# Cross-attention keys as a split product in rows, copied and turned, in place of an fp32 product

## The chip, the cores and the metric

The kernel runs on one core of one Trainium2 chip. The metric is the device time of one launch in microseconds (us), as the median of several runs. The engines are named as the profile names them: PE (TensorE; PEld is its weight loads), DVE (VectorE), ACT (ScalarE), POOL (GpSimd) and SP (SyncE, which issues most DMAs).

## The reference

```python
x = x + cross_attn(layernorm(x), ctx_1024, key_bias, key_mask, Wq, Wkv, out_w)   # 16 heads of 32, softmax over keys
x = x + self_attn(layernorm(x), Wq, Wk, Wv, Wo)       # 128 tokens; q, k, v, weights and outputs clipped to [1e-7, 1 - 1e-7]
x = x + experts(layernorm(x), gate_w, w1, w2)         # each of 8 experts picks 32 of 128 tokens; 512 -> 2048, gelu, -> 512
```

x is 4 x 128 x 512 in fp32, the context 4 x 2048 x 512. In the cross-attention, keys are `ctx @ Wk.T + bk` and values `ctx @ Wv.T + bv`. The padded tail of each batch's context is masked out.

## The kernel before, in words

The program has one hand-written instruction list for each engine, with semaphores between them. Every engine executes its own list in order, so an instruction that waits holds everything behind it on its engine.

The work goes in three parts: an **opening** (layer norm, query projection, splitting of weights), a **chunk loop** over blocks of 128 context rows (with this mask and `ctx_s` loaded 11 times, 11 chunks are needed), and then the self-attention and the experts. Chunk 0 is written out, chunks 1 to 8 run in a hardware loop (`Fori(1, prev)`), chunk 9 (`prev`, with `at_end=True`) is written out with extra normalisations between its steps, and chunk 10 (`last`) is interleaved with the output projection.

Most products are **split products**. A factor a is stored as a_hi (rounded to fp32r, by ACT, in `w_hi`, `tr_hi`, `ctx_hi`) and a_lo = a - a_hi (by DVE, in `w_lo`, `tr_lo`, `ctx_lo`), and the product is three fp32r passes: hi x hi, hi x lo, lo x hi. `w_hi` and `w_lo` have four slots of a 512 x 512 weight each; `att_w` has eight places for raw weights (`wq_s, wk_s, wv_s, wo_s, sq_s, sk_s, sv_s, so_s`). Later the expert weights are loaded into the same eight places.

In the body for chunk t, PE's list (`chunk` in the tensor block) runs:

- `k_project(t + 1)`: the keys of the next chunk. 16 fp32 matmuls of 128 columns, weight stationary, so the keys come out with the head dimension on the partitions, in the PSUM bank `pk`.
- `turn_values(t)`: four transposes of the previous chunk's output, copied by ACT to `ot_s`.
- `v_project(t + 1, k)` for k = 0 to 3: three fp32r matmuls of 512 columns each into the PSUM bank `pv`, a split product with `ctx_hi`/`ctx_lo` stationary. Between them `turn_probs(t, c)`, transposes of the exponentials.
- `scores(t + 1)`: bias matmuls (L1395) and 16 small products (L1400), then `values(t)` (L1420).

DVE's list for chunk t: `maximum(t, nm, 0)`, `maximum(t, nm, 1)` (row maxima of the scores, L908), `v_evacuate(t)` (L843, it frees `pv` for `v_project(t + 1)`), `split_chunk(t + 1)` (L849, `ctx_lo`), `moved_maxima` (L916, L918), `k_evacuate(t + 1)` (L854, adds the bias and writes `kt_s`), `add_values` (L937), `turned_probs` (L930) for c = 0, 1, then `rescale` (L925), `turned_probs` for c = 2, and `add_sums`. `scores(t + 1)` overwrites the banks that `turned_probs` reads, so it waits for the third of these (`pt_dve`) and for ACT's copy (`pt_act`). `v_project(t + 1, 0)` waits for `v_out`, which `v_evacuate(t)` raises.

ACT's list for chunk t: `split_chunk(t + 1)` (L543, `ctx_hi`, waits for `v_mm`, the end of the previous `v_project`), `turned_out`, 16 exponentials (L488) and `turned_last`.

Of the kernel before, what the change touches and what calls it, by code (L numbers as in the profile page):

```python
# [38 lines left out]
def decoder_layer(nc, x, ctx_t, key_bias, key_mask, wq, wk, wv, bv, wo, bo, bias_cols,  # L39
                  sq, sk, sv, sbv, so, sbo, gate, w1, w2, out):  # L40
    with ExitStack() as ctx:
# [11 lines left out]
        ot_s = att_w[:, 6, 0].rearrange("p (k t) -> p k t", k=KC)  # L53
# [126 lines left out]
        att_hi_ok = sem("att_hi_ok"); att_lo_ok = sem("att_lo_ok")  # L180
# [21 lines left out]
        norm_hi_ok = sem("norm_hi_ok"); norm_lo_ok = sem("norm_lo_ok"); last_lo_ok = sem("last_lo_ok"); last_mm = sem("last_mm"); last_out = sem("last_out"); last_resid = sem("last_resid"); ones_ok = sem("ones_ok"); resid_ok = sem("resid_ok"); first_hi_ok = sem("first_hi_ok"); first_lo_ok = sem("first_lo_ok");  spread_ok = sem("spread_ok")  # L202
# [10 lines left out]
        x_now_ok = sem("x_now_ok"); xin_hi_ok = sem("xin_hi_ok"); xin_staged = sem("xin_staged"); back_staged = sem("back_staged")  # L213
# [5 lines left out]
        SPLITS = ((wv_s, 1, in_wv), (sv_s, 3, in_sv), (wo_s, 2, in_wo), (sq_s, 1, in_sq), (sk_s, 0, in_sk), (so_s, 1, in_so))  # L219
# [70 lines left out]
        def _(sp):  # L290
# [45 lines left out]
            for i in range(2 * NQ):  # L336
# [4 lines left out]
                if i == 6:  # L341
                    sp.wait_ge(bt_mm, last + 1)
# [20 lines left out]
        def _(pool):  # L363
# [42 lines left out]
            g.memset(ones[:], 1.0).then_inc(ones_ok, 1)  # L406
# [64 lines left out]
        def _(act):  # L471
# [114 lines left out]
            split_att(3)  # L586
# [5 lines left out]
            split_att(4)  # L592
# [5 lines left out]
            split_att(5)  # L598
# [164 lines left out]
        def _(dve):  # L763
# [124 lines left out]
            part_split(1, 0, 2)  # L888
# [957 lines left out]
```

## Time and profile before

| | |
|---|---|
| median of 3 runs | 454.85 us (454.65 to 454.88) |
| the profiled execution, its own time | 455.0 us |
| its span, first to last instruction | 453.3 us |
| granted TensorE clock, mean | 0.996 of full |
| PE busy | 437.7 us, 97% |
| DVE busy | 367.4 us, 81% |
| ACT busy | 302.1 us, 67% |
| POOL busy | 86.9 us, 19% |
| one iteration of the chunk loop | 11.11 us |

Busy shares are averages over the whole span. The time outside of the span is 1.7 us. What a change in one part is worth is read from that part: which wait ends last there.

### The profile page before, as it was taken

How to read it: one execution, taken by the hardware profiler on the slowest of the kernel's cores; microseconds unless marked ns; L12 is line 12 of the kernel's file. 1: busy time of each engine (PE TensorE's matmuls, PEld its weight loads, DVE VectorE, ACT ScalarE, POOL GpSimd, SP SyncE). 2: the span in 40 equal slices, each digit the busy share in tenths (PEclk: the TensorE clock that was granted, in tenths of full speed). 3: DMA queues.
4: the chain of work that ended last, by engine and by line, in shares of the span. 5: the costliest groups of instructions: out<-in, count | busy, mean ns of one | idle time of the engine just before them, and what ended most of it. 6: DMA issues, size and time to landing. Idle time of an engine off the chain costs nothing.

```text
span 453.3 us, 9856 instructions
## 1 busy us (share of the span) xinstructions
PE 437.7 (97%) x3424; PEld 363.9 (80%) x3424; DVE 367.4 (81%) x516; ACT 302.1 (67%) x622; POOL 86.9 (19%) x111
## 2 busy tenths in 40 slices
PE   7999999999998999999998999999999999999995
PEld 3888888888886789878877787878778787878795
DVE  6889777777778876668987989888989898998972
ACT  4557666666665643667274877787777878778852
POOL 6100000000000122000142150505041230505002
PEclk9999999999999999999998999999999999999999
DMA  8980000001010921800000499999999989999102
GB/s 257 386 296 26 25 23 23 23 23 23 23 26 22 331 99 61 269 12 3 1 0 1 161 387 387 387 387 387 384 324 353 357 310 354 298 357 300 55 1 93
DMA packets 43105, 82.02 MB, mean 181 GB/s; under 512 B 2632, under 2 KB 3784, under 8 KB 43080
## 3 DMA queue, kind: packets, MB, share of 16 engines
q1 hardware_dynamic: 41816, 81.09, 51.3%
q10 hardware_dynamic: 1264, 0.59, 0.5%
q8 instruction: 16, 0.26, 0.2%
q14 instruction: 9, 0.07, 0.0%
HBM read 80.57 MB, written 1.10 MB: 180 GB/s over the span
## 4 chain that ended last, share of the span: by engine, by line
PE 84%; DVE 9%; ACT 2%; issue 2%; DMA 1%; POOL 1%; DVEq 1%; SPq 0%; POOLq 0%
PE po L1689 18%; PE pk L1689 11%; PE pv L1689 10%; PE pk L1298 8%; PE pv L1308 5%; PE ps L1327 5%; PE po L1715 3%; PE ps L1407 3%; PE pv L1327 3%; PE ps L1452 3%; PE ps L1400 2%; PE po L1420 2%; PE pk L1327 1%; PE po L1327 1%; DMA x_s<-in_x 1%
## 5 line engine op out<-in xcount | busy, mean ns | idle before, releaser
L1234 DVE TENSOR_TENSOR w_lo<-att_w,w_hi 128x2048 fp32r<-128x2048 f32 x60 | 138.0, 2309 | 21.3 <-ACT w_hi L705 21.3
L705 ACT CAST w_hi<-att_w 128x2048 fp32r<-128x2048 f32 x60 | 115.1, 1918 | 15.5 <-PE po L1689 15.5
L488 ACT ACTIVATE big_a<-ps,negm 128x128 f32<-128x128 f32 x176 | 62.3, 396 | 0.0
L1689 PE MATMUL po<-w_hi,ht_hi 128*128 128x512 f32 (+1 forms) x128 | 50.0, 391 | 0.0
L1689 PE MATMUL po<-w_hi,ht_lo 128*128 128x512 f32 (+1 forms) x128 | 48.7, 380 | 0.0
L1689 PE MATMUL po<-w_lo,ht_hi 128*128 128x512 f32 (+1 forms) x128 | 48.6, 380 | 0.0
L1298 PE MATMUL pk<-ctx_s,att_w 128*128 128x128 f32 x352 | 42.1, 278 | 0.0
L1298 PEld LDWEIGHTS pk<-ctx_s,att_w 128*128 128x128 f32 x352 | 40.2, 192 | 1.9 <-issue 1.8
L488 ACT ACTIVATION_READ_ACCUMULATOR big_a<-ps,negm 128x1 f32 x176 | 41.4, 235 | 0.0
L908 DVE TENSOR_REDUCE mc<-ps 128x8 f32<-128x1024 f32 x22 | 26.9, 1221 | 10.4 <-PE ps L1400 10.3
L1689 PEld LDWEIGHTS po<-w_hi,ht_lo 128*128 128x128 f32 x128 | 24.0, 187 | 5.1
L1689 PEld LDWEIGHTS po<-w_lo,ht_hi 128*128 128x128 f32 x128 | 24.1, 188 | 4.4
L1689 PEld LDWEIGHTS po<-w_hi,ht_hi 128*128 128x128 f32 x128 | 24.0, 188 | 4.4
L425 POOL COPY q_now<-qk 128x512 f32 x10 | 6.1, 613 | 110.9 <-PE ps L1400 110.9
L456 POOL CAST back_now<-state 128x128 fp32r (+1 forms) x8 | 8.6, 1070 | 95.9 <-PE ps L1734 87.5
L1689 PE MATMUL pk<-w_hi,xin_hi 128*128 128x512 f32 x64 | 26.2, 409 | 0.0
L1689 PE MATMUL pv<-w_hi,xin_hi 128*128 128x512 f32 x64 | 25.9, 405 | 0.0
L1689 PE MATMUL pk<-w_hi,xin_lo 128*128 128x512 f32 x64 | 25.3, 395 | 0.0
L1689 PE MATMUL pk<-w_lo,xin_hi 128*128 128x512 f32 x64 | 25.2, 394 | 0.0
L1689 PE MATMUL pv<-w_lo,xin_hi 128*128 128x512 f32 x64 | 25.2, 394 | 0.0
L1689 PE MATMUL pv<-w_hi,xin_lo 128*128 128x512 f32 x64 | 25.2, 394 | 0.0
L1407 PEld LDWEIGHTS ps<-ident,big_a 128*128 128x128 f32 x176 | 21.2, 140 | 4.3
(348 smaller groups left out, 1023.9 us busy)
## 6 DMA issues: line engine op xcount, KB each, us to landing
att_w<-in_w SPq DMA_DIRECT2D x64, 1024.0 KB, 7.2
ctx_s<-in_ctx_t SPq DMA_DIRECT2D x11, 256.0 KB, 2.7
x_s<-in_x SPq DMA_DIRECT2D x4, 256.0 KB, 4.2
att_w<-in_wk SPq DMA_DIRECT2D x1, 1024.0 KB, 7.8
att_w<-in_wq SPq DMA_DIRECT2D x1, 1024.0 KB, 10.3
att_w<-in_wv SPq DMA_DIRECT2D x1, 1024.0 KB, 13.5
att_w<-in_sv SPq DMA_DIRECT2D x1, 1024.0 KB, 16.1
att_w<-in_wo SPq DMA_DIRECT2D x1, 1024.0 KB, 15.8
```

The costliest lines, as they stand in the source:

```text
L488: ins = a.activation(big_a[:, h], ps[:, c, g * P:(g + 1) * P], ACT.Exp, bias=negm[:, h:h + 1], accum_out=sums[:, h:h + 1])
L705: a.copy(w_hi[:, i % SLOTS], att_w[:, i]).then_inc(hi_ok, 1)
L908: v.tensor_reduce(mc[:, hs], ps[:, 2 * half:2 * half + 2].rearrange("p c (g k) -> p (c g) k", k=P), AX.X, ALU.max).then_inc(loop_dve, 1)
L1234: v.tensor_tensor(w_lo[:, i % SLOTS], att_w[:, i], w_hi[:, i % SLOTS], ALU.subtract).then_inc(lo_ok, 1)
L1298: ins = mm(pk[:, g * P:(g + 1) * P], wk_s[:, k, g * P:(g + 1) * P], ctx_s[:, k], start=k == 0, stop=k == KC - 1)
L1308: ins = mm(pv[:], c[:, k], w[:, 1, k], start=k == 0 and c is ctx_hi and w is w_hi, stop=k == KC - 1 and c is ctx_lo, skip_group_check=True)
L1327: ins = mm(dst, l, r, start=n == 0, stop=n == len(pairs) - 1, skip_group_check=True)
L1400: ins = mm(ps[:, c, g * P:(g + 1) * P], q_now[r, g], kt_s[r, g], start=False, stop=True, skip_group_check=True)
L1407: ins = nc.tensor.transpose(ps[:, c, g * P:(g + 1) * P], big_a[:, c * KC + g], ident[:])
L1452: ins = mm(banks[g], w[:, 2, k, g * P:(g + 1) * P], t[:, k], start=first and k == 0, stop=end and k == KC - 1, skip_group_check=True)
L1689: ins = mm(dst, l, r, start=start and i == 0, stop=i == len(terms) - 1, skip_group_check=True)
L1715: ins = nc.tensor.transpose(po[:, 1, c * P:(c + 1) * P], h_s[:, q % 2, c * P:(c + 1) * P], ident[:])
```

## The change

The keys of chunks 1 to 10 become a split product too. The context is now stationary and the weight moves (12 fp32r matmuls of 512 columns), so the keys come out with the context rows on the partitions. DVE copies that from `pk` to `k_rows` (a part of the place of `wq_s`), PE turns it back with four transposes into `pk` (`k_turn`), and `k_evacuate` follows as before. Chunk 0 keeps its fp32 product.

For that the key weight is split in the opening into slot 3, in the place where the self-attention's value weight was split. The high half of that weight is now made by ACT after the softmax of chunk 9, its low half by POOL (`sv_lo_ok`) in four parts. In the opening DVE's additions of the output bias to `x_s` are spread out. On DVE `split_chunk(t + 1)` moves ahead of the second `maximum`, and in SP's list the wait for `k_mm` ahead of the load of the next chunk falls away. The order of the first expert's weight loads changes.

```diff
+        k_rows = att_w[:, 0, 1]
...
-        SPLITS = ((wv_s, 1, in_wv), (sv_s, 3, in_sv), (wo_s, 2, in_wo), (sq_s, 1, in_sq), (sk_s, 0, in_sk), (so_s, 1, in_so))
+        SPLITS = ((wk_s, 3, in_wk), (wv_s, 1, in_wv), (wo_s, 2, in_wo), (sv_s, 3, in_sv), (sq_s, 1, in_sq), (sk_s, 0, in_sk), (so_s, 1, in_so))
...
                 load_bias(t)
-                sp.wait_ge(k_mm, t + 1)
                 sp.wait_ge(ctx_lo_ok, t + 1)
                 load_chunk(t + 1)
...
-            for i in range(2 * NQ):
+            for i in (1, 2, 3, 6, 0, 4, 5, 7):
+                if i == 6:
+                    sp.wait_ge(sv_lo_ok, KC)
+                if i == 0:
+                    sp.wait_ge(bt_mm, last + 1)
...
+            pool.wait_ge(att_hi_ok, 4)
+            for k in range(KC):
+                g.tensor_tensor(w_lo[:, 3, k], sv_s[:, k], w_hi[:, 3, k], ALU.subtract).then_inc(sv_lo_ok, 1)
             shifts(1)
...
             split_chunk(last)
             softmax_chunk(prev, True)
+            act.wait_ge(kr_mm, last)
+            split_att(3)
             transposed(1, 0)
...
+            def k_copy(t):
+
+                dve.wait_ge(kr_mm, t)
+                v.tensor_copy(k_rows, pk[:]).then_inc(kr_out, 1)
...
-            dve.wait_ge(in_bo, 16)
-            for b in range(B):
-                ins = v.tensor_tensor(x_s[:, b], x_s[:, b], bo_b[:], ALU.add)
-            link(ins)
             split_att(0)
+            split_att(1)
...
+            output_bias(0, 1)
...
-            part_split(1, 0, 2)
+            output_bias(1, 2)
...
                 maximum(t, nm, 0)
+                split_chunk(t + 1)
                 maximum(t, nm, 1)
                 if before is not None:
                     dve.wait_ge(pv_mm, t)
                 v_evacuate(t)
-                split_chunk(t + 1)
                 moved_maxima(t, nm)
                 if before is None:
-                    part_split(1, 2, 4)
-                k_evacuate(t + 1)
+                    output_bias(2, 4)
+                k_copy(t + 1)
                 if before is not None:
                     add_values(before, t)
                 else:
                     part_split(2, 0, 1)
                 turned_probs(t, 0)
+                k_evacuate(t + 1)
...
             def k_project(t):
-                pe.wait_ge(ctx_in, t * 16 + 16)
-                if not isinstance(t, int) or t > 0:
-                    pe.wait_ge(k_out, t)
+
+                pe.wait_ge(ctx_hi_ok, t + 1)
+                pe.wait_ge(k_out, t)
+                for w in (w_hi, w_lo):
+                    for k in range(KC):
+                        mm(pk[:], ctx_hi[:, k], w[:, 3, k], start=w is w_hi and k == 0, stop=False, skip_group_check=True)
+                pe.wait_ge(ctx_lo_ok, t + 1)
+                for k in range(KC):
+                    ins = mm(pk[:], ctx_lo[:, k], w_hi[:, 3, k], start=False, stop=k == KC - 1, skip_group_check=True)
+                ins.then_inc(kr_mm, 1)
+
+            def k_turn(t):
+
+                pe.wait_ge(kr_out, t)
                 for g in range(KC):
-                    ins = k_block(t, g)
+                    ins = nc.tensor.transpose(pk[:, g * P:(g + 1) * P], k_rows[:, g * P:(g + 1) * P], ident[:])
                 ins.then_inc(k_mm, 1)
...
                 turn_probs(t, 0)
+                k_turn(t + 1)
                 v_project(t + 1, 1)
...
             def values_project(b):
 
+                pe.wait_ge(sv_lo_ok, KC)
                 pe.wait_ge(tr_lo_ok[2], b + 1)
```

How it moves instructions, on PE, at the head of the loop's body. Before (L1298 is the key product, L1428 `turn_values`, L1308 `v_project`, L1407 `turn_probs`):

```order
L1298 MATMUL pk<-ctx_s,att_w 128x128 [waits k_out,ctx_in]
L1298 MATMUL pk<-ctx_s,att_w 128x128 x15
L1428 MATMUL po<-ident,att_w 128x128 [waits ot_out]
L1428 MATMUL po<-ident,att_w 128x128 x3
L1304 REGISTER_ALU
L1308 MATMUL pv<-w_hi 128x512 [waits v_out,ctx_lo_ok]
L1308 MATMUL pv<-w_lo,w_hi 128x512
L1308 MATMUL pv<-w_hi,w_lo 128x512
L1405 ISA
L1407 MATMUL ps<-ident,big_a 128x128 [waits p_ok]
```

The same place in the changed kernel (its lines are numbered anew: L1311 and L1314 are the key product, L1459 `turn_values`, L1339 `v_project`, L1438 `turn_probs`, L1321 `k_turn`), from the second third of the key product on:

```order
L1311 MATMUL pk<-w_lo,w_hi 128x512 x4
L1314 MATMUL pk<-w_hi,w_lo 128x512 [waits ctx_lo_ok]
L1314 MATMUL pk<-w_hi,w_lo 128x512 x3
L1459 MATMUL po<-ident,att_w 128x128 [waits ot_out]
L1459 MATMUL po<-ident,att_w 128x128 x3
L1339 MATMUL pv<-w_hi 128x512 [waits v_out,ctx_lo_ok]
L1339 MATMUL pv<-w_lo,w_hi 128x512
L1339 MATMUL pv<-w_hi,w_lo 128x512
L1436 ISA
L1438 MATMUL ps<-ident,big_a 128x128 [waits p_ok]
L1438 MATMUL ps<-ident,big_a 128x128 x3
L1321 MATMUL pk<-ident,att_w 128x128 [waits kr_out]
```

The key product now waits for both halves of the split context, and four transposes that wait for DVE's copy (`kr_out`) stand between `turn_probs(t, 0)` and `v_project(t + 1, 1)`.

On DVE, from the first maximum of a chunk to the keys, before:

```order
L911 SCALAR_TENSOR_TENSOR negm<-mc,neg_max 128x8
L908 TENSOR_REDUCE mc<-ps 128x8 [waits s_mm]
L910 REGISTER_ALU
L911 ISA [waits loop_dve]
L911 SCALAR_TENSOR_TENSOR negm<-mc,neg_max 128x8
L843 TENSOR_TENSOR v_s<-pv,bv_b 128x16x32 [waits v_mm,pv_mm]
L849 TENSOR_TENSOR w_lo<-ctx_s,w_hi 128x4x128 [waits ctx_hi_ok]
L915 ISA
L916 TENSOR_TENSOR mdiff<-negm,neg_max 128x16 [waits negm_ok]
L917 REGISTER_ALU
L918 TENSOR_TENSOR neg_max<-neg_max,negm 128x16 [waits mdiff_ok]
L854 TENSOR_TENSOR kt_s<-pk,cols 128x512 [waits k_mm]
```

And in the changed kernel (L857 is `split_chunk`, L927 and L930 `maximum`, L851 `v_evacuate`, L935 and L937 `moved_maxima`, L862 `k_copy`):

```order
L930 SCALAR_TENSOR_TENSOR negm<-mc,neg_max 128x8
L857 TENSOR_TENSOR w_lo<-ctx_s,w_hi 128x4x128 [waits ctx_hi_ok]
L927 TENSOR_REDUCE mc<-ps 128x8 [waits s_mm]
L929 REGISTER_ALU
L930 ISA [waits loop_dve]
L930 SCALAR_TENSOR_TENSOR negm<-mc,neg_max 128x8
L851 TENSOR_TENSOR v_s<-pv,bv_b 128x16x32 [waits v_mm,pv_mm]
L934 ISA
L935 TENSOR_TENSOR mdiff<-negm,neg_max 128x16 [waits negm_ok]
L936 REGISTER_ALU
L937 TENSOR_TENSOR neg_max<-neg_max,negm 128x16 [waits mdiff_ok]
L862 COPY att_w<-pk 128x512 [waits kr_mm]
```

`split_chunk` now stands ahead of the second maximum and of `v_evacuate`, and where the keys were evacuated there is the copy of the rows; the evacuation comes later, behind the first `turned_probs`.

## Rows read from the trace of the kernel before

**Rows 1.** The page, the chain that ended last, shares of the span by engine.

```profile
PE 84%; DVE 9%; ACT 2%; issue 2%; DMA 1%; POOL 1%; DVEq 1%; SPq 0%; POOLq 0%
```

**Rows 2.** Timeline of PE, one chunk: start us, length us, line, output<-inputs, [idle before].

```profile
73.27 0.40 PE L1395 MATMUL ps<-bias,ones 32*128 32x512 bf16 x4
...
75.50 3.84 PE L1298 MATMUL pk<-ctx_s,att_w 128*128 128x128 f32 x32
79.17 0.60 PE L1428 MATMUL po<-ident,att_w 128*128 128x128 f32 x4
79.53 0.47 PE L1308 MATMUL pv<-w_hi 128*128 128x512 f32 x1
...
80.31 0.60 PE L1407 MATMUL ps<-ident,big_a 128*128 128x128 f32 x4
80.66 0.48 PE L1308 MATMUL pv<-w_hi 128*128 128x512 f32 x1
...
82.57 1.04 PE L1407 MATMUL ps<-ident,big_a 128*128 128x128 f32 x8
83.36 0.47 PE L1308 MATMUL pv<-w_hi 128*128 128x512 f32 x1
...
84.38 0.40 PE L1395 MATMUL ps<-bias,ones 32*128 32x512 bf16 x4
```

**Rows 3.** Timeline of DVE, the same chunk, same columns.

```profile
74.62 1.23 DVE L908 TENSOR_REDUCE mc<-ps 128x8 f32<-128x1024 f32 x1 [1.17 <-PE ps L1400]
...
76.07 1.22 DVE L908 TENSOR_REDUCE mc<-ps 128x8 f32<-128x1024 f32 x1
...
77.53 0.69 DVE L843 TENSOR_TENSOR v_s<-pv,bv_b 128x512 f32<-128x512 f32 x1
78.14 0.68 DVE L849 TENSOR_TENSOR w_lo<-ctx_s,w_hi 128x512 fp32r<-128x512 f32 x1
...
79.37 0.69 DVE L854 TENSOR_TENSOR kt_s<-pk,cols 128x512 f32<-128x512 f32 x1 [0.25 <-PE pk L1298]
...
82.07 0.69 DVE L930 COPY big_b<-ps 128x512 f32<-128x512 f32 x1 [0.44 <-PE ps L1407]
...
83.51 0.68 DVE L930 COPY big_b<-ps 128x512 f32<-128x512 f32 x1
```

**Rows 4.** Timeline of PE: first of 12 split-product matmuls; what follows them.

```profile
145.31 0.48 PE L1327 MATMUL pv<-w_hi,tr_hi 128*128 128x512 f32 x1
...
148.18 1.03 PE L1407 MATMUL ps<-ident,big_a 128*128 128x128 f32 x8
```

**Rows 5.** Timeline of DVE, then of ACT, in the first chunk.

```profile
31.32 1.22 DVE L908 TENSOR_REDUCE mc<-ps 128x8 f32<-128x1024 f32 x1
...
34.27 1.22 DVE L884 TENSOR_TENSOR w_lo<-att_w,w_hi 128x1024 fp32r<-128x1024 f32 x1
35.40 0.69 DVE L854 TENSOR_TENSOR kt_s<-pk,cols 128x512 f32<-128x512 f32 x1
...
31.46 0.62 ACT L543 CAST w_hi<-ctx_s 128x512 fp32r<-128x512 f32 x1 [2.32 <-PE pv L1308]
```

**Rows 6.** Timeline of DVE, PE and ACT, end of the chunk before the last.

```profile
140.16 0.68 DVE L930 COPY big_b<-ps 128x512 f32<-128x512 f32 x1
...
140.91 0.40 PE L1395 MATMUL ps<-bias,ones 32*128 32x512 bf16 x4 [1.07 <-DVE big_b L930]
...
142.81 0.59 ACT L481 CAST tr_hi<-pk 128x512 fp32r<-128x512 f32 x1 [3.05 <-PE pk L1320]
```

**Rows 7.** Timeline of POOL, its first instruction after the chunk loop's.

```profile
150.47 0.55 POOL L370 TENSOR_TENSOR rstd<-rstd,minus_half 128x1 f32<-128x1 f32 x1 [19.57 <-DVE rstd L778]
```

**Rows 8.** Lines of POOL: xcount | busy us, mean ns | idle before us.

```profile
L453 POOL TENSOR_TENSOR xin_lo<-x_now,xin_hi 128x512 fp32r<-128x512 f32 x7 | 22.9, 3268 | 0.6
...
L376 POOL TENSOR_TENSOR tr_lo<-norm,tr_hi 128x512 fp32r<-128x512 f32 x3 | 3.8, 1283 | 1.8 <-DVE gsm L1186 1.8
```

More of the change, by code:

```diff
@@ L52, in decoder_layer @@
         wq_s, wk_s, wv_s, wo_s, sq_s, sk_s, sv_s, so_s = (att_w[:, i] for i in range(8))
-        ot_s = att_w[:, 6, 0].rearrange("p (k t) -> p k t", k=KC)
+        ot_s = att_w[:, 0, 0].rearrange("p (k t) -> p k t", k=KC)
+        k_rows = att_w[:, 0, 1]
         w_hi = sb("w_hi", [P, SLOTS, KC, D], F32R)
@@ L179, in decoder_layer @@
         in_wq, in_wo, in_sq, in_sk, in_sv, in_so = (sem(f"in_{n}") for n in ("wq", "wo", "sq", "sk", "sv", "so"))
-        att_hi_ok = sem("att_hi_ok"); att_lo_ok = sem("att_lo_ok")
+        att_hi_ok = sem("att_hi_ok"); att_lo_ok = sem("att_lo_ok"); sv_lo_ok = sem("sv_lo_ok")
+        kr_mm = sem("kr_mm"); kr_out = sem("kr_out")
         wq_hi_ok = sem("wq_hi_ok"); wq_lo_ok = sem("wq_lo_ok")
@@ L212, in decoder_layer @@
         tile_mm = sem("tile_mm")
-        x_now_ok = sem("x_now_ok"); xin_hi_ok = sem("xin_hi_ok"); xin_staged = sem("xin_staged"); back_staged = sem("back_staged")
+        x_now_ok = sem("x_now_ok"); xin_staged = sem("xin_staged"); back_staged = sem("back_staged")
         gelu_ok = sem("gelu_ok"); ht_mm = sem("ht_mm"); ht_hi_ok = sem("ht_hi_ok"); ht_lo_ok = sem("ht_lo_ok")
@@ L340, in _ @@
                     sp.wait_ge(att_lo_ok, 5)
-                if i == 6:
-                    sp.wait_ge(bt_mm, last + 1)
                 if i == 7:
@@ L405, in _ @@
             g.memset(neg_max[:], MASKED).then_inc(consts, 1)
-            g.memset(ones[:], 1.0).then_inc(ones_ok, 1)
+            g.memset(ones[:], 1.0).then_inc(consts, 1)
             shifts(0)
@@ L585, in _ @@
             transposed(2, 1)
-            split_att(3)
+            split_att(4)
             transposed(1, 3)
@@ L591, in _ @@
             transposed(2, 3)
-            split_att(4)
+            split_att(5)
             for c in range(KC):
@@ L597, in _ @@
                              bias=cols[:, 2, c:c + 1]).then_inc(q2_act, 1)
-            split_att(5)
+            split_att(6)
             def split_first(i, used, count=KC):
@@ L861, in _, with output_bias @@
             query_split(1)
-            dve.wait_ge(in_bo, 16)
-            for b in range(B):
-                ins = v.tensor_tensor(x_s[:, b], x_s[:, b], bo_b[:], ALU.add)
-            link(ins)
             split_att(0)
+            split_att(1)
+            def output_bias(first, end):
+                dve.wait_ge(in_bo, 16)
+                for b in range(first, end):
+                    ins = v.tensor_tensor(x_s[:, b], x_s[:, b], bo_b[:], ALU.add)
+                link(ins)
+            output_bias(0, 1)
             def queries(c):
                 dve.wait_ge(q_mm, c + 1)
-                v.tensor_scalar(q_now[:, c], ps[:, c, 0:T], cols[:, 0, c:c + 1], SCALE, ALU.add, ALU.mult).then_inc(q_first, 1)
+                v.tensor_scalar(q_now[:, c], ps[:, c, 0:T], cols[:, 0, c:c + 1], SCALE, ALU.add, ALU.mult)
                 v.tensor_scalar(qt[:, :, c], ps[:, c].rearrange("p (b t) -> p b t", b=B), cols[:, 0, c:c + 1],
@@ L1035, in _ @@
             transposed(1, 3)
-            split_att(3)
+            split_att(4)
             cross_output(3)
@@ L1050, in _ @@
             values_out(2)
-            split_att(4)
+            split_att(5)
             for c in range(KC):
@@ L1060, in split_first @@
                 v.tensor_tensor(w_lo[:, i], att_w[:, i], w_hi[:, i], ALU.subtract).then_inc(lo_ok, 1)
-            split_att(5)
+            split_att(6)
             for c in range(KC):
@@ L1385, in scores @@
                 if isinstance(t, int) and t == 0:
-                    pe.wait_ge(q_first, KC)
+                    pe.wait_ge(q_out, KC)
                 else:
@@ L1466, in _ @@
                 query_terms(w_lo, tr_hi, g, end=True).then_inc(q_mm, 1)
-            pe.wait_ge(att_lo_ok, 1)
+            pe.wait_ge(att_lo_ok, 2)
             v_project(0, 0)
             v_project(0, 1)
-            pe.wait_ge(q_first, 4)
             pe.wait_ge(q_out, 4)
@@ L1600, in gate_columns @@
             def gate_columns():
-                pe.wait_ge(ones_ok, 1)
+                pe.wait_ge(consts, 12)
                 for k in range(KC):
```

4 lines of the change are left out of this document (2 added, 2 removed).

## The prediction

> **What bounds the kernel now.** I read the page first. The chain that ended last lies on PE for 84% [rows 1], so the question in each stretch is whether PE waits. The change touches the chunk loop, so next comes the timeline of PE over one iteration. Call B the start of the bias matmuls of `scores` (L1395). They start at 73.27 and again at 84.38, so an iteration takes 11.11 us [rows 2]. In between PE has no gap that the profile marks. Last, the timeline of DVE over the same iteration: its first maximum starts at 74.62, which is B + 1.35, and DVE waits for PE three times, 1.17 us before that maximum, 0.25 before the keys and 0.44 before the second `turned_probs` [rows 3]. So PE is the bound, but DVE is close behind: with 1.9 us of waiting in 11.1 it has little room for one more instruction of 0.7 us, and most of that room is where it waits for the scores.
>
> **PE's part of the change.** Removed: 16 fp32 matmuls, from 75.50 to the next instruction at 79.17, 3.67 us [rows 2]. Added: 12 fp32r matmuls of 512 columns. The same form stands in the output projection: 12 of them from 145.31 to 148.18, 2.87 us [rows 4]. Added too: four transposes behind four others. A run of four takes 0.35 (80.31 to 80.66) and one of eight 0.79 (82.57 to 83.36) [rows 2], so four more cost 0.44. PE alone would need 11.11 - 3.67 + 2.87 + 0.44 = 10.75 us for an iteration.
>
> **DVE's part.** Added: one copy of 128x512 out of PSUM. Such instructions follow one another every 0.61 us (77.53 to 78.14) and last 0.69 [rows 3]. The third `turned_probs`, for which the next scores wait, starts 8.89 us after the first maximum (83.51 - 74.62). With the copy, 8.89 + 0.61 = 9.50, less the waits for PE that vanish, 0.25 and 0.44, gives 8.81. Both vanish: the rows of keys are ready at B + 5.1 + 0.2 and the copy's turn on DVE comes about B + 5.8; the second `turned_probs` comes about as early as PE's transposes for it. It ends 0.69 later, PE starts 0.07 behind it (140.84 to 140.91) [rows 6], and the next maximum comes at B + 1.35. That is 8.81 + 0.69 + 0.07 + 1.35 = 10.92 at most; idle times are given less than spacings show, so it can be 0.1 or 0.2 less.
>
> **The move of `split_chunk`, and the wait that it makes.** It stands ahead of the second maximum, so the keys' third pass finds `ctx_lo` at B + 1.35 + 1.45 + 0.7 = B + 3.5, while PE asks for it at about B + 2.23 + 1.9 = B + 4.1. That is free. But it also stands ahead of `v_evacuate`, which frees `pv` for `v_project(t + 1, 0)`. `v_evacuate` now ends 1.45 (first maximum, 74.62 to 76.07) + 0.61 (split) + 1.46 (second, 76.07 to 77.53) + 0.69 = 4.21 after the first maximum starts, at B + 5.56. PE used to reach this place at 79.53, B + 6.26. Now its key product starts at B + 2.23, takes 2.87, and `turn_values` 0.36 (79.17 to 79.53), so it is there at B + 5.46. It waits. How long PE takes from the end of a DVE instruction to its own start is bounded by two rows: 0.07 [rows 6] and 0.18 (84.20 to 84.38, where PE may have been busy itself) [rows 2, 3]. I take 0.1, nearer to the clean one. From there to the next bias matmuls it was 84.38 - 79.53 = 4.85, and is 5.29 with the transposes. The iteration is then 5.56 + 0.1 + 5.29 = 10.95 us. Of the three routes this one is the longest, so it sets the pace: 0.16 us less than before, not the 0.36 that PE saves. Bounds: 10.92 to 11.03 by the two latencies, and 10.75 if the route through `v_evacuate` costs less than the rows say.
>
> Eight iterations (chunks 1 to 8, from the first maximum of chunk 1 to that of chunk 9) give 8 x 0.16 = **-1.3 us**.
>
> **Chunk 0** is bound by DVE: no wait for PE stands between its second maximum and its keys [rows 5]. Three things are added there. First, `split_chunk(1)` waits for ACT's cast, which starts at 31.46 when PE has finished `v_project(0)` and ends at 32.08; DVE was free for its next instruction at 31.32, so it stands still for 0.8. Everything of the chunk is behind it: the second maximum, the row maxima that ACT needs, `v_evacuate`. Second, the copy, 0.6. Third, two additions of the output bias (2 x 0.61, and 0.1 until the last is through) in place of the half split that took 34.27 to 35.40, 1.13 [rows 5]: 0.2. Together **+1.6 us**. PE's gain is worth nothing there. The rest of the opening is a change of places of equal work: whole splits of two weights instead of one and a half, and the bias additions spread out. DVE issues the same number of elements, PE needs the value weight's low half only behind the query projection, so I take 0, with 0.3 either way.
>
> **Chunk 9** is bound by DVE too: PE waited 1.07 us for the third `turned_probs` [rows 6]. The copy adds 0.61, the wait of 0.25 before the keys (the same code in each chunk, [rows 3]) vanishes: **+0.3 us**, between 0.25 and 0.4.
>
> **Behind the loop.** ACT's cast of the self-attention's value weight (four times the elements of one that takes 0.62 [rows 5], so at most 2.5 us) goes into 3.05 us in which ACT waits for PE before 142.81 [rows 6]. If that cover were gone, the transposed output would be late by the rest. POOL makes the low half in four subtractions of 128x512. The same form took 1.28 us each in the gate's stretch and 3.27 in the experts' [rows 8]. I take 1.28: from at most 142.3 to 147.4. Queued behind them on POOL are the second layer norm's scales, first used at 150.47 [rows 7], and ACT's normalisation waits for those. Nothing waits. The loads for the first expert change only in order: 1, 2, 3 go as before, 6 and 0 a little later, and none is used before the self-attention's projections are through. SP's load of the next chunk is issued earlier, and its bytes were never waited for.
>
> **The Trainium skill on POOL.** What makes it 1.28 or 3.27 is whether DVE is at a long subtraction of two SBUF operands at the same time, as in the experts' stretch [rows 8]. "GPSIMD Engine Reference", section 8 (Key points), of the Trainium skill says that GpSimd shares its SBUF interfaces with VectorE, in contention with instructions that have two SBUF inputs. By that rule the two durations are the same instruction with and without such company. At 142 to 147 DVE mostly reads PSUM, which speaks for the short one.
>
> **The sum.** +1.6 - 1.3 + 0.3 = +0.6. The profiled execution took 455.0 (its span and 1.7 around it), so 455.6; the median of the runs lies 0.15 below that, so **455.4 us**: no change that can be measured.
>
> **Rivals.** A measurement of this kernel can tell about 0.2%, 0.9 us, from no change, so "same" is 453.9 to 455.8.
>
> 1. *The gain of PE goes through* (faster). If `v_project` does not wait for `v_evacuate` and DVE's idle times are really the larger ones, the iteration is 10.75 and eight give -2.9: 1.6 - 2.9 + 0.3 = -1.0, 453.8 us. For it: PE and DVE are within 0.2 of each other on all three routes. Against it: the wait is worked out from spacings that repeat to 0.01 in each iteration. It decides from an iteration below 10.76. Chance 0.18.
>
> 2. *The wait on `v_evacuate` eats all of it* (slower). Place: PE before `v_project(t + 1, 0)`. Price: each 0.1 us of latency or of longer DVE instructions before `v_evacuate` is 0.8 us in all. With 0.18 of latency and two hundredths more at each of the four DVE instructions the iteration is 11.1, nothing is gained, and the kernel is at 455.0 - 0.15 + 1.9 = 456.7. It decides from an iteration above 10.99. Chance 0.22.
>
> 3. *POOL's subtractions take 3.27 each* (slower). They end at 155.4, the scales are up to 4.9 late, and the time is up to 460. It decides from about 2.0 us each. For it: seven such rows. Against it: none of DVE's long subtractions is near. By the page's rule on two SBUF inputs this would happen only beside such instructions. Chance 0.04.
>
> 4. *The change does not do what it says on PE*: fp32r passes on `pk` slower than on `pv`. Nothing in the rows speaks for it, and a loop of 11.1 or more is in the second rival's time. It is counted there.
>
> The forecast has 0.56. Range: from the first rival's 453.8, with 0.3 for the opening, 453.5, to the second one's, 456.7. Faster 0.18, same 0.56, slower 0.26.
>
> **What the profile after would show.** Iteration of 10.9 to 11.0 between two L1426. Key product 2.9 us. In front of the first `v_project` (L1339) of an iteration a gap of 0.1 to 0.2, released by DVE's L851. DVE without a wait between its first maximum and the third `turned_probs`. In chunk 0 a wait of 0.8 before L857, released by ACT. About 1.6 us later than before at the first maximum of chunk 1, level at chunk 9. POOL's L432 at 1.3 us each, done before 148. Wrong would be: a gap at `v_project` of another size, a wait of PE at `k_turn`, or an opening that pays elsewhere too.

## The result: 1% slower, outside of the range

| | before | changed |
|---|---|---|
| median | 454.83 us (453.42 to 455.38, 7 runs) | 458.54 us (457.31 to 460.70, 7 runs) |
| the profiled execution, its own time | 455.0 us | 458.15 us |
| its span | 453.3 us | 456.4 us |
| granted TensorE clock, mean | 0.996 | 0.991 |

The ratio is 1.0096, 95% interval 1.0075 to 1.0118. I had forecast 455.4 us and a range up to 456.7.

To find where 3.1 us of span went, I cut both traces at five points that exist in both: the bias matmuls of chunk 0's scores, the first maximum (DVE, `mc`) of chunks 1 and 9, the bias matmuls of the last chunk, and the first `x_s<-x_s,pv` on DVE, which ends the first output projection. Each cell is a difference of two starts of the timeline.

| stretch, us | before | changed | difference | forecast |
|---|---|---|---|---|
| start to chunk 0's bias matmuls | 28.49 | 27.52 | -0.97 | 0 |
| from there to the first maximum of chunk 1 | 12.81 | 15.22 | +2.41 | +1.6 |
| eight iterations | 88.85 | 87.97 | -0.88 | -1.3 |
| first maximum of chunk 9 to the last bias matmuls | 10.76 | 11.26 | +0.50 | +0.3 |
| from there to the first `x_s` addition | 7.47 | 10.54 | +3.07 | 0 |
| the rest | 304.9 | 303.9 | -1.0 | 0 |

The first and the last line are no effect that I can tie to the change: over all kernels below the first ranges from 27.5 to 28.9 and the last from 303.4 to 305.0. They take 2 us off the difference in this pair of executions; the medians lie 3.7 apart. (One piece of the first line is the change's: it drops the early semaphore `q_first`, so that `scores(0)` waits for `q_out`, and PE stands 0.36 us for that before chunk 0's bias matmuls. It can't be told from the spread.) The loss is in two places, **before** the loop's second chunk and **behind** the loop.

**The loop is as forecast.** PE's timeline over one iteration, the counterpart of [rows 2]:

```profile
74.36 0.40 PE L1426 MATMUL ps<-bias,ones 32*128 32x512 bf16 x4
...
76.59 1.20 PE L1311 MATMUL pk<-w_hi 128*128 128x512 f32 x4
...
78.54 1.07 PE L1314 MATMUL pk<-w_hi,w_lo 128*128 128x512 f32 x4
79.45 0.60 PE L1459 MATMUL po<-ident,att_w 128*128 128x128 f32 x4
80.07 0.47 PE L1339 MATMUL pv<-w_hi 128*128 128x512 f32 x1
...
80.84 0.60 PE L1438 MATMUL ps<-ident,big_a 128*128 128x128 f32 x4
81.28 0.60 PE L1321 MATMUL pk<-ident,att_w 128*128 128x128 f32 x4
...
85.36 0.40 PE L1426 MATMUL ps<-bias,ones 32*128 32x512 bf16 x4
```

The key product takes 79.45 - 76.59 = 2.86, where it was 3.67. The next bias matmuls are 11.00 behind the last. The four transposes of `turn_values` at 79.45 needed 0.36 before the change, now the next instruction starts 0.62 behind them: that is a wait of 0.26. DVE's timeline of the same time, the counterpart of [rows 3], says for what:

```profile
75.71 1.23 DVE L927 TENSOR_REDUCE mc<-ps 128x8 f32<-128x1024 f32 x1 [1.17 <-PE ps L1431]
...
77.17 0.68 DVE L857 TENSOR_TENSOR w_lo<-ctx_s,w_hi 128x512 fp32r<-128x512 f32 x1
...
79.23 0.69 DVE L851 TENSOR_TENSOR v_s<-pv,bv_b 128x512 f32<-128x512 f32 x1
...
80.13 0.68 DVE L862 COPY att_w<-pk 128x512 f32<-128x512 f32 x1
...
83.06 0.69 DVE L949 COPY big_b<-ps 128x512 f32<-128x512 f32 x1 [0.21 <-PE ps L1438]
...
84.50 0.69 DVE L949 COPY big_b<-ps 128x512 f32<-128x512 f32 x1
```

`v_evacuate` (L851) ends at 79.92, 4.21 behind the start of the first maximum, and PE starts 0.15 later. The copy of the rows (L862) follows without a wait. One wait of 0.21 is left before the second `turned_probs`, where I had forecast none; it costs nothing, since PE's route through `v_evacuate` is the longer one.

**Chunk 0 starts late.** DVE's timeline, then ACT's, the counterpart of [rows 5]:

```profile
27.18 0.68 DVE L882 TENSOR_TENSOR x_s<-x_s,bo_b 128x512 f32<-128x512 f32 x1
30.50 1.23 DVE L927 TENSOR_REDUCE mc<-ps 128x8 f32<-128x1024 f32 x1 [2.64 <-issue]
...
31.97 0.68 DVE L857 TENSOR_TENSOR w_lo<-ctx_s,w_hi 128x512 fp32r<-128x512 f32 x1
...
30.50 0.62 ACT L549 CAST w_hi<-ctx_s 128x512 fp32r<-128x512 f32 x1 [2.37 <-PE pv L1339]
```

The scores' last matmuls start at 27.74 and take 1.07, so PE was done at 28.8; the maximum starts at 30.50. The row gives 2.64 us of idle time to "issue": behind 28.8 it waited for nothing on another engine. The view of the chain between 27 and 31 us (start, length, what) shows DVE's own sequencer (DVEq) at work:

```profile
27.27 0.61 DVE x_s L882
...
27.90 0.55 DVEq L271
...
28.81 0.30 DVEq L274
...
29.40 0.48 issue
29.88 0.30 DVEq L266
...
30.50 1.24 DVE mc L927
```

Lines 266 to 274 are the loads of the chunk numbers into registers (`last_chunk(dve)`, `chunk_before_last(dve)` and one of the chunk's own). They begin only when the addition of the output bias (L882) is through. In the kernel before, the same loads stood behind a half split without a wait, and the first maximum came 1.37 us behind the bias matmuls; now it is 2.98.

**Behind the loop DVE stands still where it has next to nothing to do.** DVE, POOL and PE, around the end of chunk 9:

```profile
140.02 0.69 DVE L944 TENSOR_TENSOR state<-state,alpha 128x512 f32 x1 [0.52 <-issue]
...
142.10 1.29 DVE L964 TENSOR_TENSOR total<-total,sums 128x16 f32 x1
...
145.27 1.11 DVE L930 SCALAR_TENSOR_TENSOR negm<-mc,neg_max 128x8 f32<-128x8 f32 x1
146.30 0.68 DVE L800 TENSOR_TENSOR tr_lo<-pk,tr_hi 128x512 fp32r<-128x512 f32 x1
146.90 0.67 DVE L851 TENSOR_TENSOR v_s<-pv,bv_b 128x512 f32<-128x512 f32 x1
...
142.09 5.50 POOL L432 TENSOR_TENSOR w_lo<-att_w,w_hi 128x512 fp32r<-128x512 f32 x4 [10.63 <-ACT w_hi L483]
...
143.32 1.81 POOL L432 TENSOR_TENSOR w_lo<-att_w,w_hi 128x512 fp32r<-128x512 f32 x1
...
141.97 0.39 PE L1426 MATMUL ps<-bias,ones 32*128 32x512 bf16 x4 [1.69 <-DVE big_b L949]
...
147.03 0.66 PE L1351 MATMUL pk<-ident,norm 128*128 128x128 f32 x4 [2.18 <-DVE tr_lo L800]
...
147.88 0.63 PE L1358 MATMUL pv<-w_hi,tr_hi 128*128 128x512 f32 x1
...
152.31 0.93 PE L1438 MATMUL ps<-ident,big_a 128*128 128x128 f32 x7
```

Two instructions of 128x16 and 128x8 elements (L964, L930) take 1.29 and 1.11 us; in the loop's iterations each takes 0.17. POOL runs its four subtractions at that time, until 147.59. The second row of POOL shows the second of them alone: it takes 1.81, the other three 1.27 or 1.28 (in windows that hold one each). It began at 143.32, 0.01 behind DVE's multiplication of two SBUF operands (L975, 143.31, 0.68 long), so POOL stands for DVE just as DVE stands for POOL. `tr_lo` of the first output projection is late, and PE stands for 2.18 us. PE's stand of 1.69 before it is over at 141.97, before POOL begins; it was 1.07 before the change, and is 1.70 without POOL's work (experiment 1). Behind both stands PE's matmuls take 0.63 instead of 0.47. The windows of both kernels (busy time and count of each engine, granted clock, DMA), before first:

```profile
148.00:153.00 5.00, 5.00 (x33) 4.31 (x32) 4.08 (x12) 3.99 (x19) 0.74 (x2) 1.00 0.85 264
...
148.00:153.00 5.00, 5.00 (x21) 4.02 (x20) 2.32 (x6) 4.70 (x26) 0.00 (x0) 0.66 0.73 216
```

The granted clock of 148 to 153 is 0.66, a mix of the 2.4 GHz level and of the 1.2 GHz level; before it was 1.00. The 12 matmuls of the projection take 152.31 - 147.88 = 4.43, against 2.87 [rows 4]. So in this execution +3.07 is 1.5 of held DVE instructions and 1.56 of slower clock.

### The profile page after: what moved, and what is told of

Read it like the earlier page. It is cut to its first block, busy times and chain, and to the rows that moved or that the text cites. A ratio compares the mean times of both kernels' runs of the same rounds, so it can differ in the third digit from the quotient of the medians.

```text
span 456.4 us, 9538 instructions
## 1 busy us (share of the span) xinstructions
PE 437.6 (96%) x3264; PEld 355.5 (78%) x3264; DVE 373.7 (82%) x525; ACT 304.1 (67%) x623; POOL 93.1 (20%) x115
## 4 chain that ended last, share of the span: by engine, by line
PE 85%; DVE 9%; issue 2%; DVEq 1%; ACT 1%; DMA 1%; POOL 0%
PE po L1721 18%; PE pk L1721 11%; PE pv L1721 10%; PE pv L1339 5%; PE ps L1358 5%; PE pk L1311 4%; PE pv L1358 4%; PE po L1747 3%; PE ps L1438 3%; PE po L1358 2%; PE ps L1484 2%; PE po L1451 2%; PE ps L1431 2%; PE pk L1314 2%; DVE mc L927 1%
## 5 line engine op out<-in xcount | busy, mean ns | idle before, releaser
L927 DVE TENSOR_REDUCE mc<-ps 128x8 f32<-128x1024 f32 x22 | 26.8, 1220 | 12.1 <-PE ps L1431 9.4
L1438 PEld LDWEIGHTS ps<-ident,big_a 128*128 128x128 f32 x176 | 21.2, 140 | 4.3
L1438 PE MATMUL ps<-ident,big_a 128*128 128x128 f32 x176 | 24.4, 272 | 0.0
L456 POOL COPY x_now<-qk 128x512 f32 x7 | 16.2, 2320 | 38.3 <-PE pv L1721 38.3
```

The source lines that it names most:

```text
L456: g.tensor_copy(x_now[:], now).then_inc(x_now_ok, 1)
L927: v.tensor_reduce(mc[:, hs], ps[:, 2 * half:2 * half + 2].rearrange("p c (g k) -> p (c g) k", k=P), AX.X, ALU.max).then_inc(loop_dve, 1)
L1438: ins = nc.tensor.transpose(ps[:, c, g * P:(g + 1) * P], big_a[:, c * KC + g], ident[:])
```

## The experiments

Call the stretch from the last bias matmuls to the first `x_s` addition the tail. Two theories of it stood first. A: POOL's subtractions hold small DVE instructions, and the clock falls because PE then stands. C: POOL costs nothing, and what is lost is lost elsewhere, for instance by ACT's new cast. (B in an expectation is the other theory of that experiment alone.) For the opening: the sequencer's loads behind the wait, or the forecast's three terms being larger than worked out. All ratios are to the kernel before on the same chip, and experiments on different chips are compared by their ratios (the changed kernel has 1.0096). The stretches are those of the table above, from one profiled execution each.

**1. No work on POOL.** The low half of the self-attention's value weight is left out (POOL only signals).

```diff
-                g.tensor_tensor(w_lo[:, 3, k], sv_s[:, k], w_hi[:, 3, k], ALU.subtract).then_inc(sv_lo_ok, 1)
+                pool.sem_inc(sv_lo_ok, 1)
```

> The changed kernel without POOL's four subtractions behind the chunk loop: the low half of the self-attention's value weight is left out (what stands in its slot is used), everything else stays. Theory A (POOL's subtractions hold up DVE's small instructions with two SBUF operands, and the longer wait of PE that follows drops the granted clock): L964 and the L930 that follow it at the last chunk take 0.17 us again, not 1.29 and 1.11; PE's wait before the second L1351 of the tail falls from 2.18 to about 0.7; the clock at the first output projection is 1.00 and its 12 matmuls take 2.8, not 4.35. From the last chunk's bias matmuls to the end of that projection 7.5, not 10.5; in all about 3 us less, 455.5. Theory B (the clock falls there for another reason): 1.5 less, the 4.35 stay. Theory C (POOL costs nothing, the time is lost in opening and loop): no change within 0.5.

455.69 us, ratio 1.0032 (1.0019 to 1.0045). DVE at the same place:

```profile
142.84 0.17 DVE L964 TENSOR_TENSOR total<-total,sums 128x16 f32 x1
...
145.44 0.17 DVE L930 SCALAR_TENSOR_TENSOR negm<-mc,neg_max 128x8 f32<-128x8 f32 x1
```

The tail is 7.47, to the hundredth what it was before the change, with the cast of ACT still in it. Theory C falls: the whole of +3.07 hangs on POOL's work, and the ratio falls by 0.0064, 2.9 us.

**2. POOL's work in the kernel before.** ACT casts another weight into slot 3 behind chunk 9's softmax and POOL makes its low half, for which `values_project` waits (so the self-attention's values come from another weight); the rest of the change is left out, but for `q_first`, which goes here too (chunk 0 keeps its place: 28.46 and 12.80 in the first two stretches).

```diff
             softmax_chunk(prev, True)
+            act.wait_ge(in_so, 16)
+            act.wait_ge(att_lo_ok, 3)
+            a.copy(w_hi[:, 3], so_s).then_inc(again_hi, 1)
...
+            pool.wait_ge(again_hi, 1)
+            pool.wait_ge(att_lo_ok, 3)
+            for k in range(KC):
+                g.tensor_tensor(w_lo[:, 3, k], so_s[:, k], w_hi[:, 3, k], ALU.subtract).then_inc(again_lo, 1)
...
             def values_project(b):
+                pe.wait_ge(again_lo, KC)
```

> The kernel before with this part alone: ACT casts a weight into slot 3 after the softmax of chunk 9 and POOL makes the low half in four subtractions of 512 columns behind the chunk loop, awaited by the values' projection. (The weight is the self-attention's output weight, since the other one is overwritten by then, so the values of the self-attention are others.) Opening and loop as before. Theory A (this part costs about 3 us by itself, 1.5 through DVE and 1.5 through the clock): 457.5 or so, with DVE instructions of 1.1 to 1.3 at the last chunk and the first output projection at 4.35; if POOL's start falls so that a DVE instruction escapes, 1 us. Theory C (it costs nothing without the rest of the change): level with before.

454.72 us, ratio 1.0003 (0.9988 to 1.0018): a miss for theory A's 457.5, and in time what theory C had said, "level with before". The tail is 7.87, only 0.4 more. POOL's and DVE's rows:

```profile
141.59 5.00 POOL L430 TENSOR_TENSOR w_lo<-att_w,w_hi 128x512 fp32r<-128x512 f32 x4 [10.74 <-ACT w_hi L576]
...
143.58 0.56 DVE L918 SCALAR_TENSOR_TENSOR negm<-mc,neg_max 128x8 f32<-128x8 f32 x1
```

POOL does the same work, yet one instruction is held, for 0.4. What differs is when POOL begins: at 141.59 DVE was already inside its 0.68 us multiplication of two SBUF operands (L963), behind its small additions. In the changed kernel POOL began at 142.09, 0.01 ahead of L964. So I took the price to be no constant, but what is left of POOL's current subtraction when such a DVE instruction comes. The next run tests that.

**3. POOL begins 0.3 us later.**

```diff
             pool.wait_ge(att_hi_ok, 4)
+            pool.wait_ge(total_ok, 10)
```

> The changed kernel with one thing more: POOL begins its four subtractions only when DVE has done the last small addition of the last chunk but one (total_ok, L964), some 0.3 us later. Nothing else moves. Phase theory (what a held instruction of DVE costs depends on where in POOL's current subtraction it starts): L964 takes 0.17 instead of 1.29, so everything on DVE behind it is 1.1 us earlier; the small negm (L930) then starts near the end of POOL's second subtraction or early in the third, hold 0.3 to 1.2; tail (bias matmuls of the last chunk to the first x_s addition) between 7.9 and 9.3 us instead of 10.54, the granted clock at 1.00 where PE's waits are below 2 us; time 455.5 to 457.5. Rival (the price is POOL's work as such, whenever it starts): the tail stays at 10.2 to 10.8, time 458.5.

456.86 us, ratio 1.0057 (1.0039 to 1.0074). The tail is 7.86, where the changed kernel had 10.54:

```profile
143.23 0.18 DVE L965 TENSOR_TENSOR total<-total,sums 128x16 f32 x1
143.32 0.68 DVE L976 TENSOR_TENSOR norm<-state,norm_c 128x512 f32<-128x512 f32 x1
...
145.83 0.56 DVE L931 SCALAR_TENSOR_TENSOR negm<-mc,neg_max 128x8 f32<-128x8 f32 x1
...
143.56 5.29 POOL L433 TENSOR_TENSOR w_lo<-att_w,w_hi 128x512 fp32r<-128x512 f32 x4 [10.96 <-DVE total L965]
```

L965 (the same addition) takes 0.18, and the multiplication behind it, begun 0.24 ahead of POOL, its usual 0.68. `negm` at 145.83 takes 0.56 and ends at 146.39: POOL's second subtraction, alone in its window, runs from 145.09 for 1.28, to 146.37. The same holds in the changed kernel: POOL's third runs from 145.09 for 1.27, to 146.36, and `negm` ends at 146.38; the first ends at 143.36, and L964 at 143.39. `tr_lo` comes 3.21 behind the last bias matmuls, where it was 4.33, and the granted clock stays at 1.00. POOL's ends are rough, so this holds to a tenth. A start of POOL that is later by 0.3 us gives back 2.7 in the tail (forecast: 1.2 to 2.6), and 1.8 by the ratios.

**4. POOL in 16 pieces of 128 columns.**

```diff
-                g.tensor_tensor(w_lo[:, 3, k], sv_s[:, k], w_hi[:, 3, k], ALU.subtract).then_inc(sv_lo_ok, 1)
+                for q in range(4):
+                    now = slice(q * P, (q + 1) * P)
+                    ins = g.tensor_tensor(w_lo[:, 3, k, now], sv_s[:, k, now], w_hi[:, 3, k, now], ALU.subtract)
+                ins.then_inc(sv_lo_ok, 1)
```

> The changed kernel with POOL's low half in 16 subtractions of 128 columns in place of 4 of 512. Theory A (a DVE instruction with two SBUF operands that starts while POOL is inside a subtraction stands until that subtraction ends): DVE's small instructions at the last chunk are held for at most the length of one short subtraction, 0.3 to 0.5, not 1.1 to 1.3; PE's wait before the second L1351 falls to about 1.0, and the clock stays up, so that from the last chunk's bias matmuls to the end of the first output projection it takes 7.7 to 8.5 instead of 10.5; in all about 2 us less. Theory B (DVE is held until POOL has done all of its queue): the long instructions stay.

456.92 us, ratio 1.0048 (1.0032 to 1.0063). The tail is 7.78:

```profile
143.15 7.23 POOL L434 TENSOR_TENSOR w_lo<-att_w,w_hi 128x128 fp32r<-128x128 f32 x16 [10.64 <-ACT w_hi L486]
...
143.16 0.48 DVE L967 TENSOR_TENSOR total<-total,sums 128x16 f32 x1
...
145.76 0.47 DVE L933 SCALAR_TENSOR_TENSOR negm<-mc,neg_max 128x8 f32<-128x8 f32 x1
```

POOL needs 7.23 us in place of 5.50, and the hold shrinks with the piece: 0.48 and 0.47, with POOL again 0.01 ahead of the same addition. A hold costs 0.3 here, in a place where it had cost 1.1.

**5. Keep PE's clock.** Six and eight matmuls on constants, into a bank that nobody reads then, go in front of the last chunk's scores and behind the values of chunk 9.

```diff
+                if at_end:
+                    pe.wait_ge(summed, t)
+                    keep_warm(6, 7)
                 scores(t + 1)
...
                 values(t)
+                if at_end:
+                    keep_warm(8, 7)
```

> The changed kernel with matmuls that fill PE's two longest waits at the loop's end, 6 of 512 columns before the last chunk's bias matmuls and 8 behind the values of the chunk before; their results are not used. POOL's subtractions stay. Theory A (the clock falls because PE stands still for 1.7 and 2.2 us): the granted clock stays 1.00 from 148 to 153, the first output projection takes 2.8 us instead of 4.35, about 1.5 less in all, and DVE's two long small instructions stay at 1.1 to 1.3. Theory B (the clock falls for another reason): 4.35 stays, no change or a little more time.

457.85 us, ratio 1.0076 (1.0055 to 1.0097). The window of the projection:

```profile
148.00:153.00 5.00, 4.65 (x30) 3.97 (x29) 3.88 (x8) 5.00 (x29) 1.00 (x1) 1.00 0.47 125
```

The clock is 1.00, the tail 8.98 = 10.54 - 1.56, and the held instructions of DVE are as they were. So the two halves of the profiled +3.07 are separate: 1.5 for the late `tr_lo`, 1.56 for the clock. Two things stay unshown. The medians do not confirm the second half: the ratio fell by 0.0020, 0.9 us, for the 1.5 that I had expected, and the intervals overlap. The seven runs of the changed kernel have mean clocks from 0.986 to 0.996, and one at 0.996 took 458.88 where one at 0.990 took 457.31. And that standing brings the clock down is not shown by this run alone: in experiment 10 PE stands as long, and the clock stays.

**6. No wait behind the bias additions.**

```diff
-                link(ins)
+                ins.then_inc(dchain, 1)
+                links[0] += 1
```

> The changed kernel with the output bias's additions followed by no wait of DVE for their own end (the semaphore is raised, a later wait covers it). Theory A (the loads of chunk numbers stand behind that wait and take 2.6 us, uncovered): the first maximum of chunk 0 starts 1.4 us after its bias matmuls instead of 3.0, but then the wait of 0.8 for ACT's cast before L857 comes back, so the first maximum of chunk 1 is only about 0.8 earlier counted from the bias matmuls (14.4, not 15.2): 0.8 us less in all. Theory B (the loads are slow wherever they start): the first maximum stays 3.0 behind, no change.

455.22 us, ratio 1.0023 (1.0009 to 1.0037). The first maximum of chunk 0 is back at 1.36 behind the bias matmuls, and the wait that I had forecast appears:

```profile
32.24 0.69 DVE L857 TENSOR_TENSOR w_lo<-ctx_s,w_hi 128x512 fp32r<-128x512 f32 x1 [0.72 <-ACT w_hi L549]
...
144.49 0.56 DVE L931 SCALAR_TENSOR_TENSOR negm<-mc,neg_max 128x8 f32<-128x8 f32 x1
```

The stretch is 14.27: 0.95 better, because 1.6 at the maximum comes back and 0.7 of it goes into the wait for ACT. It gained more in all than the 0.8 or so expected, 3.3 us by the ratios. DVE's idle time of 0.52 before L944 at the end of chunk 9 is 0.13 here, as in the kernel before. POOL's start does not hang on it (it waits for ACT's cast), so L964's addition (L965 here, 141.89) comes 0.37 ahead of POOL (142.26) where it had come 0.01 behind. One `negm` of 0.56 is held, and the tail is 7.87. This is the kind moment of experiment 3, reached by another way: a gap of 0.39 us on DVE's sequencer decides over 2.7 us of the tail. More than half of the gain has nothing to do with the opening.

**7. And `split_chunk` behind `v_evacuate` in chunk 0 alone.** Experiment 6 with:

```diff
                 maximum(t, nm, 0)
-                split_chunk(t + 1)
+                if before is not None:
+                    split_chunk(t + 1)
                 maximum(t, nm, 1)
...
                 v_evacuate(t)
+                if before is None:
+                    split_chunk(t + 1)
```

> The changed kernel without the wait behind the output bias (as in e2) and with split_chunk behind v_evacuate in chunk 0 alone. Theory A: the wait of 0.72 for ACT's cast in chunk 0 goes, so from the first bias matmuls to the first maximum of chunk 1 13.6 us instead of 14.3 (before 12.8; 0.6 of the rest is the copy and 0.2 the bias additions); 0.7 less than e2. Theory B (PE becomes the bound in chunk 0 without it): 14.3 stays.

453.86 us, ratio 0.9990 (0.9975 to 1.0005). The stretch is 13.63, another 0.64 less. What is left against 12.81 is 0.82: the copy and the additions.

**8. `v_evacuate` ahead of the second maximum,** in all chunks, all else as changed.

```diff
                 split_chunk(t + 1)
-                maximum(t, nm, 1)
                 if before is not None:
                     dve.wait_ge(pv_mm, t)
                 v_evacuate(t)
+                maximum(t, nm, 1)
```

> The changed kernel with v_evacuate ahead of the second maximum on DVE (chunks 0 to 9). Theory A (an iteration is set by PE's wait for v_evacuate at the first v_project): the gap before the first L1339 goes, an iteration falls from 11.00 to between 10.75 and 10.9, in all 1 to 2 us less. Theory B (DVE's chain to the third turned_probs sets the iteration): 11.00 stays, since DVE's sum is the same.

457.85 us, ratio 1.0080 (1.0052 to 1.0107). PE's timeline in one iteration:

```profile
79.33 0.60 PE L1459 MATMUL po<-ident,att_w 128*128 128x128 f32 x4
79.68 0.48 PE L1339 MATMUL pv<-w_hi 128*128 128x512 f32 x1
...
84.97 0.40 PE L1426 MATMUL ps<-bias,ones 32*128 32x512 bf16 x4
```

The next instruction follows `turn_values` by 0.35: no wait. An iteration takes 10.735, the 10.75 of PE alone. The 2.1 us of eight iterations hardly reach the median (the ratio fell by 0.0016, with overlapping intervals; 1 to 2 us were expected). The tail is 9.82, with three small instructions of 1.1 to 1.2 us, and chunk 9 takes 11.37. Here PE stands for 2.05 before the last bias matmuls, and the granted clock is 0.50 from 142 to 145, at another place than in the changed kernel.

**9. All together.** Experiments 4, 6, 7 and 8 in one kernel, with `maximum(t, nm, 1)` ahead of `v_evacuate` in chunk 0.

> The changed kernel with the edits of e4, e5 and e6 together: no wait behind the output bias, chunk 0 with split_chunk last, v_evacuate ahead of the second maximum, POOL in 16 pieces. If they add up: opening 13.6, iteration 10.74, chunk 9 about 11.0, the stretch to the end of the first output projection 8: against the kernel before +0.8 - 3.0 + 0.2 + 0.5 = -1.5 us, 453.2, faster by 0.3%. The rival: the savings in the opening are eaten by a lower clock or a new wait, and it ends level with the kernel before.

**452.44 us** (4 runs), ratio 0.9946 (0.9925 to 0.9967): 0.5% less than the kernel before. The opening stretch is 13.47, the iteration 10.736, chunk 9 10.97, the tail 7.76.

**10. The same with POOL in four subtractions again.** The edit of experiment 4 is taken out.

> The combined kernel (no wait behind the bias additions, split_chunk behind v_evacuate in chunk 0, v_evacuate ahead of the second maximum elsewhere) with POOL's low half in 4 subtractions of 512 columns again instead of 16 of 128. Theory that the pieces are what protects the tail: holds of up to 1.2 us on DVE's small instructions come back, the tail is 8.5 to 10.5 instead of 7.76, time 453.5 to 455. Rival (in this kernel POOL starts at a kind moment, as in the two kernels without the bias wait and the old order of v_evacuate): one hold of about 0.5, tail 7.9, time 452.4 to 452.8, the same as with 16 pieces.

453.84 us, ratio 1.0001 (0.9984 to 1.0017):

```profile
138.05 1.77 DVE L976 TENSOR_TENSOR norm<-state,norm_c 128x512 f32<-128x512 f32 x1
...
141.10 1.11 DVE L931 SCALAR_TENSOR_TENSOR negm<-mc,neg_max 128x8 f32<-128x8 f32 x1
...
137.97 5.44 POOL L432 TENSOR_TENSOR w_lo<-att_w,w_hi 128x512 fp32r<-128x512 f32 x4 [10.36 <-ACT w_hi L483]
...
137.83 0.40 PE L1430 MATMUL ps<-bias,ones 32*128 32x512 bf16 x4 [1.66 <-DVE big_b L950]
...
142.86 0.66 PE L1355 MATMUL pk<-ident,norm 128*128 128x128 f32 x4 [2.15 <-DVE tr_lo L800]
...
142.00:147.00 5.00, 4.14 (x24) 3.56 (x25) 3.88 (x9) 4.76 (x27) 1.41 (x2) 1.00 0.23 83
```

POOL begins 0.08 ahead of the multiplication, which takes 1.77 in place of 0.68, and `negm` is held to the end of the third subtraction (140.92 + 1.26 = 142.18; `negm` ends at 142.21). The tail is 8.94, 1.18 more than with 16 pieces. The ratios differ by 0.0055, 2.5 us, and their intervals do not overlap.

The last three rows are a test of the clock that I had not planned. PE stands for 1.66 and for 2.15 us, as in the changed kernel (1.69 and 2.18, in the same 6.7 us), yet the granted clock stays at 1.00 over the projection. So two such stands are not enough to bring the clock down; what else it takes is open. It is also a second measurement of the DVE half: 8.94 - 7.47 = 1.47 with the full clock.

## Why the prediction was wrong, step by step

- **PE alone, 10.75**: right. The key product took 2.86 for 2.87; without the wait the iteration is 10.735.
- **The route through `v_evacuate`, 10.95**: the mechanism and every spacing were right, 4.21 to the hundredth, 5.29 behind it. The term that was mis-sized is PE's latency, taken at 0.1 and measured at 0.15. That makes 11.00, and -0.88 for -1.3. Between 0.07 and 0.18 I had leaned on one row; the other was nearer.
- **Chunk 0, +1.6**: the three terms are right: 0.72 for the wait (0.8 forecast), 0.82 for the copy and the additions (0.8 forecast); experiments 6 and 7 separate them.
- **"The rest of the opening ... I take 0, with 0.3 either way"**: failed. I counted DVE's elements and not what its sequencer has to do behind a wait. The last of the moved additions put `link` ahead of the register loads. They cost 1.6 at the first maximum, less the 0.7 that then no longer had to be waited for ACT: +0.9. "DVE issues the same number of elements" was true and not the point.
- **Chunk 9, +0.3**: +0.50. 0.12 of it are the change (experiment 6: 10.88 for 10.76). The other 0.38 come with a gap of the sequencer before L944 (`140.02`, 0.52 on issue, for 0.13 before), the same that puts L964 behind POOL's start. It stands in the six kernels that have the wait behind the bias additions and in none of the four that do not; why a wait at 27 us should leave a gap at 140 stays open.
- **"Behind the loop. ... Nothing waits"**: the step that failed most. Of POOL's duration I was right (1.27 or 1.28 in three of four, and 1.81 where it began behind DVE's multiplication; all done at 147.59), also that ACT's cast is hidden (the tail of experiment 1). But I asked only whether POOL would be slowed by DVE, and who waits for POOL. I never asked what POOL does to DVE, which at 142 to 147 has small instructions with two SBUF operands on the path to `tr_lo`. That costs 1.5 in the changed kernel. In the profiled execution 1.56 more go to a fall of the clock, which is absent when POOL has no work and when PE's stands are filled, but also in experiment 10 with the stands in place. My third rival named POOL, with the wrong mechanism. That the tail costs so much in the changed kernel and 0.4 in four of the others is luck of phase, which the rows of before did not let me work out.
- The sum: the forecast's +0.6 with what each stretch missed, 0.8 + 0.4 + 0.2 + 3.1, makes +5.1, which is 2.41 - 0.88 + 0.50 + 3.07. The first and last stretch, which vary between executions, took 2 of them back in the profile.

The Trainium skill has the rule that I missed. "SBUF — State Buffer", section "Who interferes with whom", says that a VectorE instruction with two SBUF inputs contends with a GpSimd instruction that reads SBUF, that the shared ports are an exclusive lock and the order of issue decides who stands, and that a VectorE instruction with at most one SBUF input, outside of the two-port modes, does not take part. The rows here agree: `v_s<-pv,bv_b` at 146.90, which has one operand in PSUM and began 0.59 behind POOL's fourth subtraction, takes its 0.67 beside it; the multiplication that began ahead of POOL takes 0.68 (experiment 3) and the one that began behind it 1.77 (experiment 10); and POOL's subtraction that began 0.01 behind a multiplication takes 1.81. The lock lasts to the end of the other's instruction, within 0.04 us for the small ones. I had cited "GPSIMD Engine Reference", section 8 (Key points), which names the contention and not its direction, and had read it for POOL's side alone.

## What to carry to other kernels

Work given to an idle GpSimd is not free because nobody waits for its result: while it reads SBUF, each VectorE instruction with two SBUF operands can stand for the rest of GpSimd's current instruction, and the other way round. Look for small ones on the path, and cut GpSimd's work into short pieces, so that the price hangs less on a start that may shift by some tenths of a microsecond. When work is moved past a wait on one's own engine, ask what the sequencer does behind it (register loads, table reads), since it is no longer hidden by the queue. And a change that shifts a phase can gain or lose more elsewhere than by its own edit, so cut both traces into stretches before crediting an edit with the change of the total.

## What the runs showed of the hardware

- A DVE operation of two SBUF operands of 128x8 or 128x16 elements, 0.17 us, took up to 1.29 beside POOL's subtractions of 128x512 (1.26 to 1.30 each when not held), and 0.38 to 0.48 beside those of 128x128 (0.45 each). One of 128x512, 0.68, took 1.77. POOL's own took 1.81 where it began 0.01 behind DVE's multiplication.
- After PE had stood for 1.69 and 2.18 us within 7 us, 12 matmuls took 4.43 us for 2.87, at a granted clock of 0.66 in that window; with 14 matmuls put into the stands it was 1.00. After stands of 1.66 and 2.15 us in experiment 10 it was 1.00 too.
- The loads of three numbers into DVE's registers, with nothing queued ahead to hide them, took from 27.90 to 30.46, 2.6 us, 0.48 of it "issue" between them.
- Open: the gap of 0.52 before L944, as said above; what besides the two stands brings the clock down; and why the experiments' medians differ by up to 1 us more or less than their stretches; the stretch behind the first output projection alone varies by 1.5 between executions.
